# A fused attention and mixture-of-experts kernel: the fourth block's attention after the experts, and expert 0 between the second and third block

## The reference

```python
x = L0_attn_x                                  # (4, 512, 128) fp32
xn = layernorm(x)
y = xn @ U                                     # (4, 512, 32), attention
dist_sq = n_i + n_j - 2 * (y @ y.T)            # n = sum(y * y)
att = softmax(-dist_sq) @ xn                   # per batch
shared = (silu(xn @ sg) * (xn @ su)) @ sd      # sg, su: 128x1024; sd: 1024x128
# routed: 8 experts, the top 2 per token, at most 320 slots per expert
rw = top2(softmax(rms_norm(xn) @ router_w.T)), normalized over the two
routed[token] += rw * (silu(xg @ rg[e]) * (xg @ ru[e])) @ rd[e]
out = x + att + shared + routed
```

## Time and profile before

| | |
|---|---|
| median of three runs | 156.9 us |
| profiled execution | 156.88 us, its span 155.4 us |
| granted TensorE clock | 1.00 |
| busy: TensorE / its weight loads | 150.5 / 135.1 us |
| busy: VectorE / ScalarE / GpSimd | 117.4 / 103.5 / 83.2 us |
| chain that ended last | TensorE 92%, VectorE 2%, DMA 2%, ScalarE 1%, GpSimd 1% |

### The profile page before, as it was taken

How to read it: one execution, slowest core, us unless ns; L and a number is a source line. 1 busy time by engine, 2 the same in 40 slices (tenths; PEclk the granted TensorE clock), 3 DMA queues, 4 the chain that set the end, 5 groups by cost and what they waited for, 6 DMA issues and landing times.

```text
span 155.4 us, 3117 instructions
## 1 busy us (share of the span) xinstructions
PE 150.5 (97%) x964; PEld 135.1 (87%) x964; DVE 117.4 (76%) x290; ACT 103.5 (67%) x217; POOL 83.2 (54%) x102
## 2 busy tenths in 40 slices
PE   6999999999999999999999999999999999999992
PEld 6878777889999888888888899999999999878991
DVE  3999969899735599998988777786786786546871
ACT  3369999999469397768756569889677466334100
POOL 7653422357777787877400005698988847454000
PEclk9999999999999999999999999999999999999999
DMA  4999999981111117435069300423232011118486
GB/s 128 302 275 111 210 308 343 343 245 54 55 53 51 51 54 218 158 80 172 0 173 259 124 0 2 152 58 98 67 103 72 25 46 34 30 32 291 96 273 186
DMA packets 26638, 20.72 MB, mean 133 GB/s; under 512 B 2333, under 2 KB 22840, under 8 KB 26624
## 3 DMA queue, kind: packets, MB, share of 16 engines
q1 hardware_dynamic: 24544, 17.76, 42.4%
q0 software_dynamic: 1792, 2.65, 5.6%
q10 hardware_dynamic: 288, 0.14, 0.3%
HBM read 12.36 MB, written 7.92 MB: 131 GB/s over the span
## 4 chain that ended last, share of the span: by engine, by line
PE 92%; DVE 2%; DMA 2%; ACT 1%; POOL 1%; issue 1%; DVEq 0%
PE bank L1259 9%; PE bank L1344 9%; PE bank L1179 8%; PE bank L1181 8%; PE bank L1180 8%; PE bank L1290 8%; PE bank L1284 8%; PE bank L1287 8%; PE bank L1400 5%; PE bank L1402 5%; PE bank L1401 5%; PE bank L1416 2%; PE bank L1244 2%; PE bank L1427 2%; DMA acc<-in_L_attn_x_dram 2%; PE bank L1199 1%
## 5 line engine op out<-in xcount | busy, mean ns | idle before, releaser
L673 ACT ACTIVATE silu<-bank 128x512 f32<-128x512 f32 (+1 forms) x64 | 33.3, 520 | 29.5 <-PE bank L1290 28.9
L567 POOL DMA_INDIRECT slots_dram<-row,slot_i x32 | 34.0, 1063 | 10.9 <-issue 9.4
L1010 DVE TENSOR_TENSOR bank<-bank,silu 128x320 f32<-128x320 f32 (+1 forms) x48 | 27.1, 565 | 15.5 <-ACT silu L673 12.6
L586 POOL DMA_INDIRECT routed_dram<-eo,xg x24 | 23.0, 957 | 11.5 <-DVE eo L1050 6.3
L1016 DVE TENSOR_TENSOR hid_lo<-bank,hid_hi 128x320 fp32r<-128x320 f32 (+1 forms) x48 | 26.2, 546 | 0.0
L681 ACT CAST hid_hi<-bank 128x320 fp32r<-128x320 f32 (+1 forms) x48 | 22.9, 477 | 0.0
L574 POOL TENSOR_TENSOR ew_lo<-sw_raw,ew_hi 128x1024 fp32r<-128x1024 f32 x3 | 7.2, 2414 | 19.3 <-ACT ew_hi L697 19.3
L1010 DVE TENSOR_TENSOR hid_s<-bank,silu 128x512 f32<-128x512 f32 x16 | 11.0, 686 | 5.6 <-PE bank L1181 5.2
L1344 PEld LDWEIGHTS bank<-sd,hid_s 128*128 128x128 f32 x128 | 14.8, 192 | 0.3
L1259 PEld LDWEIGHTS bank<-row,probs 128*128 128x128 f32 x128 | 14.8, 191 | 0.2
L1344 PE MATMUL bank<-sd,hid_s 128*128 128x128 f32 x128 | 15.0, 275 | 0.0
(11 more groups left out here) (204 smaller groups left out, 362.6 us busy)
## 6 DMA issues: line engine op xcount, KB each, us to landing
sw_raw<-in_L_ffn_rg_dram SPq DMA_DIRECT2D x8, 256.0 KB, 3.1
sw_raw<-in_L_ffn_ru_dram SPq DMA_DIRECT2D x8, 256.0 KB, 3.6
rd_raw<-in_L_ffn_rd_dram SPq DMA_DIRECT2D x8, 256.0 KB, 3.4
routed_dram<-fill SPq DMA_DIRECT2D x1, 2048.0 KB, 11.7
routed<-routed_dram SPq DMA_DIRECT2D x8, 256.0 KB, 4.1
slots_dram<-fill SPq DMA_DIRECT2D x1, 1300.0 KB, 12.2
xg<-slots_dram SPq DMA_DIRECT2D x8, 130.0 KB, 2.4
row<-row SPq DMA_DIRECT2D x1, 1024.0 KB, 7.7
```

Of the source, the lines that this page charges most:

```text
L567: G.indirect_dma_start(slots_dram, bass.IndirectOffsetOnAxis(slot_i[:, k, t:t + 1], 0), row[:, t, 0:RW], None, bounds_check=E * CAP - 1, o ...
L673: C.activation(silu[:, q % 2, 0:n], gate_bank(q)[:, 0:n], ACT.Silu).then_inc(silu_ready, 1)
L1010: V.tensor_tensor(hid, up[:, 0:n], silu[:, q % 2, 0:n], ALU.mult).then_inc(hid_ready, 1)
```

## The change

The fourth block's `scores`, `exps` and `attend` leave the front. The scores now stand within the last chunk of block 3, the exponentials at the end of ScalarE's program, and the two halves of `attend` within `down_end_block`; `add_attention` stands before the last block sum. Their PSUM banks and the buffer for the probabilities are others, and one of the buffers for rounded down weights moves to a part of the token buffer, as block 3's scores now keep theirs. The order of jobs becomes block 0, block 1, expert 0, block 2, experts 1 to 7, block 3. GpSimd sorts each token's two experts by number, so that `row1` belongs to the lower one; all 16 rows of `row1` are scattered first, and SyncE loads expert 0's slots after these 16. The slots of experts 0 and 1 are transposed after chunk 6 of blocks 1 and 2 and split in chunk 7. The diff is cut to what matters here:

```diff
-SPREAD = ()
-ORDER = [("block", b, c) for b in range(EARLY) for c in range(CS)]
-for e in range(E):
-    ORDER += [("expert", e, c) for c in range(CR)]
-    if e in SPREAD:
-        ORDER.append(("block", B - 1, SPREAD.index(e)))
-ORDER += [("block", B - 1, c) for c in range(len(SPREAD), CS)]
+JOBS = [("block", 1), ("expert", 0), ("block", 2)] + [("expert", e) for e in range(1, E)]
+ORDER = [(*job, c) for job in [("block", 0)] + JOBS + [("block", B - 1)]
+         for c in range(CS if job[0] == "block" else CR)]
...
-    rd_hi, rd_lo = [t[:, CS * D:CS * D + 2 * CR * D].rearrange("p (s c d) -> p s c d", s=2, c=CR)
-                    for t in (yL, yR)]
+
+    rd_hi, rd_lo = [[in_y[:, CS * D:CS * D + CR * D].rearrange("p (c d) -> p c d", c=CR),
+                     in_x[:, 0:CR * D].rearrange("p (c d) -> p c d", c=CR)]
+                    for in_y, in_x in ((yL, xnT_hi), (yR, xnT_lo))]
+
+    end_probs = sw_raw[:, :, :].rearrange("p s (j i) -> p (s j) i", i=S)
+
+    def probs_of(b):
+        return end_probs if b == B - 1 else probs[:, b % 2, :, :]
...
+    end_score_b = [bank[7], bank[4], bank[5], bank[6]]
+    end_down_b = [bank[0], bank[1]]
+    end_att_b = [bank[2], bank[3]]
+
+    def score_bank(b, j):
+        return end_score_b[j] if b == B - 1 else bank[j]
+
+    def att_bank(b, h):
+        return end_att_b[h] if b == B - 1 else down_b[h]
...
         for e in range(2, 5):
             next_expert_weights(e)
             next_down(e)
-        sp.wait_ge(scattered, 16 * 2 * NT)
-        sp.wait_ge(xg_padded, 1)
-        load_slots(0)
+            if e == 2:
+                sp.wait_ge(scattered[0], 16 * NT)
+                sp.wait_ge(xg_padded, 1)
+                load_slots(0)
+        sp.wait_ge(scattered[1], 16 * NT)
         load_slots(1)
...
+            sp.wait_ge(att_added, 2 * (B - 1) + h + 1)
...
         def route_places():
-
-            pool.wait_ge(later_ready, 1)
-            after(G.tensor_scalar(later_i[:, :], later[:, :], float(T), None, ALU.mult))
-            G.tensor_tensor(row1[:, :, 1].bitcast(I32), place_i[:, 0, :], later_i[:, :], ALU.add)
-            after(G.tensor_tensor(row2[:, :, 1].bitcast(I32), place_i[:, 1, :], later_i[:, :], ALU.subtract))
+            G.tensor_copy(row1[:, :, 1].bitcast(I32), place_i[:, 0, :])
+            after(G.tensor_copy(row2[:, :, 1].bitcast(I32), place_i[:, 1, :]))
...
+            G.tensor_scalar(top_w[:, :], th[:, :], -0.5, 0.5, ALU.mult, ALU.add)
+            after(G.tensor_tensor(shares[:, :, :], swaps[:, 0:2, :],
+                                  e2[:, :].rearrange("p (o t) -> p o t", o=1).to_broadcast([P, 2, NT]), ALU.mult))
+            after(G.tensor_tensor(shares[:, :, :], shares[:, :, :], swaps[:, 1:3, :], ALU.add))
+            G.tensor_tensor(row1[:, :, 0], top_w[:, :], shares[:, 0, :], ALU.mult)
+            after(G.tensor_tensor(row2[:, :, 0], top_w[:, :], shares[:, 1, :], ALU.mult))
+
+        def route_in_order():
+
+            pool.wait_ge(second_ready, 1)
+            after(G.tensor_tensor(behind[:, :], i1, i2, ALU.subtract))
+            after(G.tensor_scalar(behind[:, :], behind[:, :], 0.0, None, ALU.max))
+            G.tensor_tensor(in_order[:, 0, :], i1, behind[:, :], ALU.subtract)
+            G.tensor_tensor(in_order[:, 1, :], i2, behind[:, :], ALU.add).then_inc(order_ready, 1)
+
+        def route_swaps():
+
+            G.tensor_scalar(swaps[:, 0, :], behind[:, :], 1.0, None, ALU.min)
+            after(G.tensor_scalar(swaps[:, 2, :], behind[:, :], 1.0, None, ALU.min))
+            after(G.tensor_scalar(swaps[:, 1, :], swaps[:, 0, :], -1.0, 1.0, ALU.mult, ALU.add))
 
         route_gap()
-        pool.wait_ge(second_ready, 1)
-        G.tensor_scalar(ends[:, :, :], experts[:, :, :], float(CAP), float(CAP), ALU.mult, ALU.add
+        route_in_order()
+        pool.wait_ge(order_ready, 1)
+        G.tensor_scalar(ends[:, :, :], in_order[:, :, :], float(CAP), float(CAP), ALU.mult, ALU.add
                         ).then_inc(ends_ready, 1)
+        route_swaps()
         route_places()
...
-        for t in range(NT):
-            for k, row in enumerate((row1, row2)):
+        for k, row in enumerate((row1, row2)):
+            for t in range(NT):
                 G.indirect_dma_start(
                     slots_dram, bass.IndirectOffsetOnAxis(slot_i[:, k, t:t + 1], 0), row[:, t, 0:RW], None,
-                    bounds_check=E * CAP - 1, oob_is_err=False).then_inc(scattered, 16)
+                    bounds_check=E * CAP - 1, oob_is_err=False).then_inc(scattered[k], 16)
 
         def split_weights(e):
...
+        write_routed(0)
         for e in range(E):
             if e + EW < E:
                 split_weights(e + EW)
-            write_routed(e)
+            if e > 0:
+                write_routed(e)
...
+                if j == 0 and b == B - 1:
+                    act.wait_ge(ew_split_pool, E - DVE_WEIGHTS)
+                elif j == 0 and b >= 2:
                     act.wait_ge(att_done, 2 * (b - 1))
-                C.activation(probs[:, b % 2, j, :], bank[j][:, :], ACT.Exp, scale=2.0
+                C.activation(probs_of(b)[:, j, :], score_bank(b, j)[:, :], ACT.Exp, scale=2.0
...
                 elif c == 6:
                     round_down_weights(2)
+                else:
+                    slots_hi(0)
...
-                elif c == 6:
-                    slots_hi(0)
+                elif c == 7:
+                    slots_hi(1)
             elif kind == "expert":
-                if c == 1 and i + 1 < E:
+                if c == 1 and 1 <= i < E - 1:
                     slots_hi(i + 1)
                 if c in (0, 1) and i >= 1 and i + EW - 1 < E:
                     round_weights(i + EW - 1, c)
                 if c == 3 and i >= 1 and i + RD - 1 < E:
                     round_down_weights(i + RD - 1)
+        exps(B - 1)
...
         def route_order():
-            V.tensor_tensor(later[:, :], i1, i2, ALU.is_gt).then_inc(later_ready, 1)
+            dve.wait_ge(order_ready, 1)
+            dve.wait_ge(sel_ready, 1)
+            mark(V.tensor_tensor(chosen[:, :, :, :], ids_twice, experts_in_order, ALU.is_equal))
...
                 else:
                     split_weights(2, c - 6)
+                    if c == 7:
+                        slots_lo(0)
...
-                elif c == 6:
-                    slots_lo(0)
-            elif kind == "expert" and c == 1 and i + 1 < E:
+                elif c == 7:
+                    slots_lo(1)
+            elif kind == "expert" and c == 1 and 1 <= i < E - 1:
                 slots_lo(i + 1)
...
+        dve.wait_ge(block_added, B)
+        add_attention(B - 1, 0)
+        add_attention(B - 1, 1)
+        dve.wait_ge(att_added, 2 * B)
         end_block_sum(1)
...
+            elif b == B - 1:
+                pe.wait_ge(eo_ready, E)
+                pe.wait_ge(hid_ready, len(ORDER) - 2)
+                pe.wait_ge(xg_ready, E)
+                pe.wait_ge(out_copied, len(JOBS))
             for j in range(TG):
                 if b == 0:
                     pe.wait_ge(hid_ready, CS)
-                else:
+                elif b < B - 1:
...
+            elif b == B - 1:
+                pe.wait_ge(hid_ready, len(ORDER))
...
-            first, second = turn_b[0], sums_b
-            pe.wait_ge(xg_ready, E)
-            pe.wait_ge(hid_ready, at["block", b, CS - 2])
+            first, second = end_down_b
+            pe.wait_ge(silu_ready, at["block", b, CS - 1])
+            pe.wait_ge(hid_ready, at["block", b, CS - 1])
             down_tile(first[:, 0:D], 0, range(CS - 2))
-            pe.wait_ge(out_copied, len(JOBS))
             down_tile(second[:, 0:D], 2, range(CS - 2))
             pe.wait_ge(hid_ready, at["block", b, CS - 1] + 1)
             down_tile(first[:, 0:D], 0, range(CS - 2, CS))
             down_tile(first[:, D:2 * D], 1).then_inc(end_down, 1)
+            attend(b, 0)
+            attend(b, 1)
             down_tile(second[:, 0:D], 2, range(CS - 2, CS))
             down_tile(second[:, D:2 * D], 3).then_inc(end_down, 1)
...
-        scores(3)
         attend(2, 1)
-        attend(3, 0)
-        attend(3, 1)
...
+                between = None
+                if q == CLOSE:
+                    between = lambda: down_chunk(END)
+                elif q == len(ORDER) - 1:
+                    between = lambda: scores(B - 1)
+                up_of_block(i, c, between)
...
-            if (kind, i, c) == ("block", EARLY - 1, 5):
-                turn_slots(0)
-            elif kind == "expert" and c == 0 and i + 1 < E:
+            if kind == "block" and i in WIDE and c == CS - 2:
+                turn_slots(i - 1)
+            elif kind == "expert" and c == 0 and 1 <= i < E - 1:
                 turn_slots(i + 1)
```

More of the change, by code:

```diff
@@ L75, in moe_attention_kernel @@
     LAG = 3
-    JOBS = [("block", b) for b in WIDE] + [("expert", e) for e in range(E)]
     END = at["expert", E - 1, CR - 1]
@@ L147, in moe_attention_kernel @@
```

(27 more changed lines are left out.)

27 lines of the change are left out of this document (13 added, 14 removed).

## The result

The changed kernel takes 161.2 us (median; 161.1 to 162.75 in six runs) against 156.95 us for the kernel before on the same chip: ratio 1.0283, 95% interval 1.0243 to 1.0322. It is slower by 4.25 us; the forecast was 160.4 us, +3.49.

The account below looks back on a forecast made before the run. TensorE's matmuls, 97% of the span, were taken to bound the kernel. Front +0.25 and boundaries +3.24, all else 0, gave +3.49 us on 156.88: forecast 160.4 us, own range 159.4 to 161.4, with 158.3 to 161.9 holding 8 of 10.

Parts of the forecast that it names:

- TensorE bounds the kernel: Whole span: TensorE is 97% busy, so moving matmuls wins only idle time, some 0.1 us in the middle and the tail.
- Routing in front: VectorE's wait for the sorted pair and one longer compare delay the first scores: +0.25 us, bounds 0 and +0.7.
- Expert 0's rows: Slots on the chip at about 58.5 us, transposes at 60.0 us: margin 1.5 us, cost 0.
- The two boundaries: Second block to expert 0, third to expert 1: TensorE waits for slots_lo in VectorE's queue, 1.92 and 1.32 us.
- Moved attention: Fourth block's scores and attention: 4.50 us leave the front and return at the end, net 0, bounds -0.1 to 0.
- end waits: Exponentials before the last attention: at most 3.4 us, covered by 5.6 us of TensorE's work, cost 0.
- tail: After TensorE's last matmul: last sum and store landing, about 2.9 us, change taken as 0, bounds -0.5 and 0.
- The clock falls in the pauses: Rival at the new pauses: the 1.2 GHz level returns, +2.0 us per pause, 162.3 to 164.3 us; chance 0.06.
- TensorE's pace fixed at 0.23 us: All of TensorE: one 512-column matmul starts every 0.23 us, whatever the load on other engines.
- 1.5 us around the span: Time of the profiled execution outside its span: 156.88 us against a span of 155.4.
- a rival in which the pace rises: All 512-column matmuls: fewer neighbours' accesses save 4.8 us at most, 155.6 us at full; chance 0.08, half of it faster.

Follow-up runs that it names:

- e6: The kernel of e1 with the new small tiles behind the old ones, so every other tile lies where it lay before: 157.68 us, ratio 1.0015.
- e8: The kernel before with only the routing of the change (GpSimd sorts the pair, VectorE marks both experts in one compare): 157.56 us.
- e11: The kernel of e8 with the sorted order of the scatters too, all rows of the lower experts first: 157.45 us, ratio 0.9999.
- e12: The kernel before with the last attention moved to the end and nothing else of the change: 165.74 us, ratio 1.0538.
- e2: The changed kernel with slots_lo ahead of the split of expert 2's weights, in the second block's chunk 7 only: 160.74 us, ratio 1.0211.
- e1: The changed kernel with the slots' steps ahead of the last chunk's silu on ScalarE and product on VectorE: 158.0 us, ratio 1.0042.
- e4: The kernel before with unused tiles of 320 and 128 bytes where the change puts its new small ones: 157.25 us, ratio 0.9997.

## Why the prediction was right, point by point

- *TensorE bounds the kernel, so a move alone wins nothing.* Right: with both queues mended and the tiles in place (e6) the kernel has all of the change but its two pauses, and measures 0.4 us over the one before, which its interval does not tell from the same; it is not faster.
- *Routing in front, +0.25 us.* Right in sign, in part in mechanism, too large: 0.15 us in the trace, 0.11 to 0.14 in comparison of like stretches. Counted from `sel`, the compare made 0.07 of it (the start of `n_lo`); the other 0.06 is `slot_i`, which takes 0.25 to 0.26 us in after, e8 and e11 and 0.19 to 0.20 in the traces of before, and which my sum did not have. Why it is slower is not shown. The compare took 0.43 us where I took 0.50, and it began at 27.89 us where I had about 28.0. The last of GpSimd's steps starts at 27.63 and takes 0.22 us, so the sorted pair was there at 27.85, as reckoned (27.9).
- *Expert 0's rows, margin 1.5 us, cost 0.* The cost was right. The margin was smaller: the loads were issued at 56.40 and 56.77 us, not 55.6, because the 16th scatter, at 52.37 us, took 1.42 us where I had about 1. They had landed at 59.60 us, and the transposes came at 60.40 where I had 60.0: a margin of 0.8 us. I did not say what e12 shows: that the sorted order is what pays for the moved attention at all.
- *The two boundaries, 1.92 + 1.32 us.* Right, and most of the result: 1.97 + 1.37 us. Taken away one operation at a time they shrink as the chain says (e2: 0.60 us), and taken out of the queue they vanish (e1). Each was 0.05 us more than reckoned, the time from the end of `slots_lo` to TensorE's start being 0.10 to 0.11 us where I took 0.05. What I left out is the expert's slow first step behind each pause, 0.15 us for both; with it the pauses cost 3.49 us, which is what TensorE gets back in e1 (123.57 - 120.07 = 3.50).
- *Moved attention, 0; end waits, 0; tail, 0.* Right within 0.1 us for TensorE's work (e12), and no wait for the exponentials. Block 1 starts at 47.72 us, 4.34 us earlier than before, where I had 4.25. The tail reads 0.02 us longer by the span; by the landing of the last store it is 0.24 us longer, of which 0.13 are the two additional waits that I had at nothing. By the span it is 2.95 us, where I had given 2.4 to 2.9 as the sign.
- *The clock falls in the pauses* (rival, 2.0 us each). Wrong for these pauses, whose clock stayed at 1.00. The price was right in the one pause that did bring the clock down (e12, of 5.6 us): 2.04 us. The Trainium skill, TensorE: Matmul & The Clock Gate, "Why this matters for your kernels", warns that a gap in mid-kernel brings the lower level back. The trace of e12 agrees (granted clock 0.50); in the pauses of 1.97 and 1.37 us it stayed at 1.00.
- *TensorE's pace fixed at 0.23 us.* The term that I mis-sized, with its sign against me: I had a rival in which the pace rises and none in which it falls. It went from 231 to 233 ns. All 512-column steps sum up to 56.96 us without the pauses, against 56.55 before: 0.41 us, of which 0.39 stand from the first scores on. With the 0.15 us of the slow first steps that is nearly all of the 0.60. The places of the tiles account for 0.17 to 0.33 us of it (e6, e4).
- *1.5 us around the span.* Taken as fixed, it read 1.73 in the trace. That is the earlier end of the span, not a cost; the cost stands in the tail, above.

So the sum of the mechanisms named was 3.49 us and measured 3.49 (0.15 + 3.34), the front 0.10 too large and the pauses 0.10 too small. That they cancel to the hundredth is luck. The 0.8 us by which the forecast fell short are TensorE's steps outside the pauses (0.60) and its end (0.23), which I had carried over unchanged, and 161.2 us lies in the range.

## What to carry to other kernels

When a job moves next to another, read the in-order queues of the helper engines at the new seam: an operation that only waits for old data may stand behind one that waits for the newest, and the price is that chain, one step for each operation. When work is taken out ahead of something, ask also whose cover it was: a stream with its own pace (here the scatters) does not come earlier with the rest. Before two profiled spans are subtracted, look at which event ends each of them. And keep the places of old tiles when new ones are added, or measure what a shift alone costs.

## What the runs showed of the hardware

- TensorE's pace depends on where tiles lie: nine 512-column matmuls take 2080 ns with the tiles in their old places (the commonest value in eight of eight traces, once 2081) and 2100 ns with them shifted by 320 and 128 bytes (six of six).
- A pause of 1.97 us left the granted clock at 1.00; in one of 5.6 us it fell to 0.50, and after it the low clock cost 2.04 us.
- The profiled span does not end at a fixed distance from the end of the measured time: 0.63 us behind the last store's landing in six traces, 0.41 in eight, with 2.11 to 2.15 us from that landing to the end of the measured time in thirteen of fourteen.
